# The experts' first layer with its weights standing in TensorE, and marks and gates made ahead

## The reference, cut to what matters

```python
gate_logits = einsum('bnd,ed->ben', x, gate_query)
affinity = _sinkhorn(gate_logits / exp(log_temp))      # 6 rounds
gates, idx = top_k(affinity, CAP)                      # CAP = 64 tokens for each of 16 experts
expert_in = take_along_axis(x[:, None], idx[..., None], axis=2)
h = gelu(einsum('becd,edf->becf', expert_in, w1) + b1[None, :, None, :])   # FF = 1024
expert_out = einsum('becf,efd->becd', h, w2) + b2[None, :, None, :]
out = zeros_like(x).at[batch, idx].add(gates[..., None] * expert_out)
```

## Time and profile before

| | |
|---|---|
| Median of 3 runs | 1174.94 us (1174.15 to 1175.01) |
| The profiled execution's own time | 1175.17 us |
| Its span, first to last instruction | 1173.4 us |
| Mean granted clock of TensorE | 0.976 |
| Busy: PE, DVE, ACT, POOL | 94%, 73%, 61%, 13% |

### The profile page before, as it was taken

How to read it: one execution, slowest core, us unless ns; L and a number is a source line. 1 busy time by engine, 2 the same in 40 slices (tenths; PEclk the granted TensorE clock), 3 DMA queues, 4 the chain that set the end, 5 groups by cost and what they waited for, 6 DMA issues and landing times.

```text
span 1173.4 us, 30372 instructions
## 1 busy us (share of the span) xinstructions
PE 1105.5 (94%) x12600; PEld 525.7 (45%) x12600; DVE 860.9 (73%) x2017; ACT 718.2 (61%) x823; POOL 151.4 (13%) x260
## 2 busy tenths in 40 slices
PE   4788999999999999999999999999999999888997
PEld 2443433332432323544454456555555552467554
DVE  4888565487788878889788889788878980378631
ACT  0345567887678867677776877677785789310111
POOL 3024125112111011000001000010001000000522
PEclk9898999999999989999999999999999999998999
DMA  5113408722011000103232200111102000088696
GB/s 168 32 36 95 117 16 152 169 36 74 25 35 40 16 15 2 53 28 88 79 101 65 88 18 28 52 47 30 30 20 65 17 16 2 24 310 193 184 345 173
DMA packets 81562, 90.45 MB, mean 77 GB/s; under 512 B 18208, under 2 KB 73952, under 8 KB 81424
## 3 DMA queue, kind: packets, MB, share of 16 engines
q1 hardware_dynamic: 75264, 80.04, 23.9%
q10 hardware_dynamic: 4368, 6.29, 1.7%
q0 software_dynamic: 1792, 2.16, 1.0%
HBM read 73.42 MB, written 15.04 MB: 75 GB/s over the span
## 4 chain that ended last, share of the span: by engine, by line
PE 76%; DVE 11%; DMA 5%; issue 4%; ACT 2%; POOL 1%; ACTq 0%; DVEq 0%; POOLq 0%
PE po L1778 24%; PE g L1886 16%; PE scores L1754 15%; PE scores L1758 6%; PE g L1871 3%; PE g L1831 2%; ACT probs L1194 2%; DMA out<-self_region,idx_scatter 1%; DVE mx L1465 1%; PE g L1821 1%; PE g L1861 1%; DMA out<-wo_sb,idx_scatter 1%; PE scores L1787 1%; DMA out<-wxq_sb,idx_scatter 1%; PE g L1977 1%
## 5 line engine op out<-in xcount | busy, mean ns | idle before, releaser
L1194 ACT ACTIVATE probs<-scores 128x1024 f32<-128x1024 f32 (+2 forms) x736 | 677.0, 968 | 239.7 <-PE scores L1754 131.3
L1465 DVE TENSOR_REDUCE mx<-g 128x1 f32<-128x400 f32 (+1 forms) x1024 | 526.4, 567 | 86.2 <-PE g L1886 76.6
L1886 PE MATMUL g<-cross_region,even_region 96*32 96x400 bf16 (+1 forms) x4096 | 310.5, 338 | 0.4
L1754 PE MATMUL scores<-even_region,cross_region 99*32 99x512 bf16 (+1 forms) x3264 | 255.0, 379 | 2.5 <-ACT probs L1194 2.5
L1778 PE MATMUL po<-probs,cross_region 128*32 128x512 f32 (+1 forms) x1664 | 225.3, 594 | 0.8 <-ACT probs L1194 0.8
L1886 PEld LDWEIGHTS g<-cross_region,even_region 96*32 96x32 bf16 x4096 | 123.3, 95 | 182.9 <-DVE mx L1465 81.9
L1778 PE MATMUL po<-probs,self_region 128*32 128x512 f32 (+3 forms) x1280 | 152.1, 550 | 4.5 <-POOL probs L1055 3.9
L1754 PEld LDWEIGHTS scores<-even_region,cross_region 99*32 99x32 bf16 (+1 forms) x3264 | 100.9, 96 | 96.0 <-issue 42.6
L1758 PE MATMUL scores<-self_region 36*128 36x512 bf16 (+3 forms) x640 | 104.9, 360 | 7.2 <-ACT probs L1194 6.8
L1055 POOL TENSOR_SCALAR_AFFINE_SELECT probs<-probs 128x256 f32<-128x256 f32 x128 | 58.8, 468 | 276.7 <-ACT probs L1194 275.9
L1022 POOL TENSOR_TENSOR rstd<-mv,half 128x1 f32<-128x1 f32 x48 | 26.7, 556 | 518.5 <-DVE mv L1273 518.3
(11 more groups left out here) (287 smaller groups left out, 881.3 us busy)
## 6 DMA issues: line engine op xcount, KB each, us to landing
cross_region<-in_w SPq DMA_DIRECT2D x16, 1024.0 KB, 12.8
even_region<-xq_d SPq DMA_DIRECT2D x192, 64.0 KB, 2.3
self_region<-in_w ACTq DMA_DIRECT2D x6, 1024.0 KB, 6.6
self_region<-in_w SPq DMA_DIRECT2D x6, 1024.0 KB, 13.8
cross_region<-xk_d SPq DMA_DIRECT2D x24, 200.1 KB, 8.0
xb<-in_x SPq DMA_DIRECT2D x32, 128.0 KB, 2.8
xb<-x_d SPq DMA_DIRECT2D x32, 128.0 KB, 2.4
probs<-in_w SPq DMA_DIRECT2D x4, 1024.0 KB, 13.2
```

The source lines that it names most:

```text
L1194: act.activation(probs[0:rows, s % 4, :, off:], ps[s % 2][0:rows, :, off:], ACT.Exp, scale=LSCALE if QUADS[n][0] == "self" else 1.0).then_ ...
L1465: dve.reduce_max(mx[:, k % 2, b, h, c:c + 1], g[:, 0:n_keys], AX_X).then_inc(g_free, 1)
L1754: mm = pe.matmul(ps[s % 2][c:c + n_keys, a, :], k_cross[0:NS * DH + 3, h, i * P + c:i * P + c + n_keys], rhs, start=True, stop=True)
L1886: mm = pe.matmul(g[q:q + 32, 0:n_keys], q_max[k % 2][0:NS * DH, h, b * P + q:b * P + q + 32], k_cross[0:NS * DH, 4 * (k % 4) + h, start:st ...
```

## The change

- `hidden(i, e)`: a 128x128 block of W1 stands in the array, and the 64 tokens of one expert stream. The output comes turned, with hidden numbers on the partitions, straight into the score bank `ps[i % 2]`. `turn_hidden` is gone.
- VectorE adds the bias from the score bank to `h_sb` in one 128x1024 instruction, with the bias on the partitions (`b1_t`); ScalarE's GELU reads `h_sb`. All biases come in one load, turned once by TensorE and copied.
- Marks: one bf16 comparison of 128x1024 for all pairs, summed by two matmuls of 512 columns. The token numbers' sums come from eight matmuls right after `tops`. `read_sums` runs once, over all pairs, and the first layer of pair 0 waits for it.
- Gates: the best values go through the same six shift steps as the token numbers, two of them ahead of the inputs, four spread between; a matmul adds the chunks up. The store of affinities and eight gathers are gone.
- `keep_busy` goes from 15 to 18 calls ahead of `best_t` and from 12 to 17 ahead of `tops`, with single ones later.
- In round i the merge of pair i−1 now stands between the two experts of the first layer. `next_w1` waits for the first layer's matmuls.

```diff
@@ tail order
-        tail += ["aff", "best_t", "cand_a", "cand_b", "limit", "sums", "tops", ("xe", 0), ("xe", 1), ("h", 0, 0), ("h", 0, 1), ("xe", 2),
-                 ("h", 1, 0), ("h", 1, 1)]
+        tail += ["aff", "best_t", "cand_a", "cand_b", "limit", "sums", "tops", "b1", ("xe", 0), ("xe", 1), ("xe", 2), "gates"]
...
@@ SP
-            for i in range(NB1):
-                if b1_sb[i] is b1_sb[-1]:
-                    sp.wait_ge(g_full, g_at(("gate", TB - 1)) + 1)
-                load_b1(i)
+            sp.dma_start(b1_rows, b1.rearrange("e (f n) -> (e f) n", n=P)).then_inc(b1_loaded, 16)
...
-            sp.wait_ge(router_pe, 3 + SINK_ITERS)
-            sp.dma_start(affin_d.rearrange("(b p) e -> p b e", p=P), affin[:, :, :]).then_inc(affin_stored, 16)
...
-                sp.wait_ge(g_free, TF["h", i, 1])
-                if i + NB1 < E // 2:
-                    load_b1(i + NB1)
+                sp.wait_ge(h_turned, i + 1)
@@ ScalarE
-                act.activation(h_t[i % 2], ps[i % 2][:, :, :].rearrange("p a b -> p (a b)"),
-                               ACT.Gelu_apprx_tanh).then_inc(gelu_done, 1)
+                act.activation(h_t[i % 2], h_sb[i % 2], ACT.Gelu_apprx_tanh).then_inc(gelu_done, 1)
@@ VectorE
+            def mark_tokens():
+                dve.tensor_tensor(marks, row_no.unsqueeze(1).broadcast_to((P, E // 2, P)),
+                                  idx_f.unsqueeze(2).broadcast_to((P, E // 2, P)), ALU.is_equal).then_inc(marked, 1)
+
+            def read_sums():
+                dve.wait_ge(pair_sums, 2)
+                link(dve.tensor_tensor(mix[:, :, 0:CAP], ps[0][:, 0, :].rearrange("p (i n) -> p i n", n=CAP),
+                                       idx_f.unsqueeze(2).broadcast_to((P, E // 2, CAP)), ALU.is_equal))
+                counts_of = ps[1][:, :, :].rearrange("p a b -> p (a b)").rearrange("p (i n) -> p i n", n=P)
+                dve.scalar_tensor_tensor(out=unused, in0=counts_of, scalar=0.0,
+                                         in1=row_no.unsqueeze(1).broadcast_to((P, E // 2, P)), op0=ALU.is_equal,
+                                         op1=ALU.mult).then_inc(sums_read, 1)
...
             def hidden(i):
-                for f in range(2):
-                    g = tail_full(dve, ("h", i, f))
-                    dve.tensor_tensor(h_sb[i % 2][:, f * TILE:(f + 1) * TILE], g[:, :],
-                                      b1_sb[i % NB1][:, f * TILE:(f + 1) * TILE], ALU.add).then_inc(g_free, 1)
+                dve.wait_ge(h_turned, i + 1)
+                if i >= 2:
+                    dve.wait_ge(gelu_done, i - 1)
+                dve.tensor_tensor(h_sb[i % 2].rearrange("p (f e n) -> p f e n", f=8, e=2),
+                                  ps[i % 2][:, :, :].rearrange("p a (f e n) -> p (a f) e n", f=4, e=2),
+                                  b1_t[:, 2 * i:2 * i + 2, :].rearrange("p e f -> p f e").unsqueeze(3)
+                                  .broadcast_to((P, 8, 2, CAP)), ALU.add).then_inc(h_biased, 1)
...
+            mark_tokens()
+            for r in range(2):
+                link(dve.memset(shifted_v[r][:, 0:CAP], 0.0))
+            link(dve.scalar_tensor_tensor(out=shifted_v[0][:, CAP:2 * CAP], in0=row_no[:, 0:CAP], scalar=n_here,
+                                          in1=best_v, op0=ALU.is_lt, op1=ALU.mult))
+            link(move(shifted_v, 0))
+            link(move(shifted_v, 1))
+            g = tail_full(dve, "b1")
+            dve.tensor_copy(b1_t.rearrange("p n f -> p (n f)"), g[:, 0:P]).then_inc(g_free, 1)
+            dve.wait_ge(g_free, TF["b1"])
             expert_in(0)
             expert_in(1)
-            mark(4)
-            mark(5)
-            read_sums(0)
+            link(move(shifted_v, 2))
+            read_sums()
             hidden(0)
-            mark(6)
-            mark(7)
             expert_in(2)
-            read_sums(1)
+            for k in range(3, 5):
+                link(move(shifted_v, k))
+            move(shifted_v, 5).then_inc(values_ready, 1)
             hidden(1)
@@ TensorE
-            keep_busy(15)
+            keep_busy(18)
             g = tail_bank(pe, "best_t")
...
-            keep_busy(12)
+            keep_busy(17)
             g = tail_bank(pe, "tops")
...
+            for i in range(E // 2):
+                mm = pe.matmul(ps[0][:, 0, CAP * i:CAP * (i + 1)], same_expert[:, 2 * i:2 * i + 1].broadcast_to((P, P)),
+                               shifted[0][:, CAP:2 * CAP], start=True, stop=True)
+            mm.then_inc(pair_sums, 1)
...
+            def hidden(i, e):
+                n = 2 * i + e
+                pe.wait_ge(w1_loaded[n % NSLOT], 16 * (n // NSLOT + 1))
+                if e == 0:
+                    pe.wait_ge(g_free, TF["xe", i])
+                    if i >= 2:
+                        pe.wait_ge(h_biased, i - 1)
+                    else:
+                        pe.wait_ge(sums_read, 1)
+                w = slots[n % NSLOT][:, 0:2048].rearrange("p (k n) -> p k n", k=DK)
                 pt = ps[i % 2][:, :, :].rearrange("p a b -> p (a b)")
                 for f in range(8):
+                    for k in range(DK):
+                        mm = pe.matmul(pt[:, f * P + CAP * e:f * P + CAP * (e + 1)], w[:, k, f * P:(f + 1) * P],
+                                       x_et[i % 2][:, k, CAP * e:CAP * (e + 1)], start=(k == 0), stop=(k == DK - 1))
+                if e:
+                    mm.then_inc(h_turned, 1)
...
             for i in range(E // 2):
-                if i + 1 < E // 2:
-                    turn_hidden(i + 1)
-                if i:
-                    merge(i - 1)
                 if i + 3 < E // 2:
                     expert_in(i + 3)
                 if i + 2 < E // 2:
-                    hidden(i + 2)
+                    hidden(i + 2, 0)
+                if i:
+                    merge(i - 1)
+                if i + 2 < E // 2:
+                    hidden(i + 2, 1)
                 expert_out(i)
```

More of the change, by code:

```diff
@@ L54 @@
 CHUNK = T // NCH
-NB1 = 5
 NONES = 8
@@ L614, in decoder_layer @@
         chunk_base = late_region[:, P + 4 * E + NCH:P + 4 * E + NCH + 1]
-        picked_affin = late_region[:, 256:256 + E // 2 * E].rearrange("p (i e) -> p i e", e=E)
+        gates = late_region[:, 256:256 + E // 2]
+        shifted_v = [even_region[:, 2304 + 2 * CAP * r:2304 + 2 * CAP * (r + 1)] for r in range(2)]
         idx_gather = sb("idx_gather", [P, E // 2], U32)
@@ L691, in decoder_layer @@
         picked = sem("picked")
-        affin_stored = sem("affin_stored")
-        gates_gathered = [sem(f"gates_gathered{i}") for i in range(E // 2)]
+        values_ready = sem("values_ready")
         gathered = [sem(f"gathered{i}") for i in range(E // 2)]
-        b1_loaded = [sem(f"b1_loaded{r}") for r in range(NB1)]
+        b1_loaded = sem("b1_loaded")
+        h_biased = sem("h_biased")
         b2_loaded = sem("b2_loaded")
@@ L961, in _ @@
                 load_w2(sp, e)
[L963 to L967, removed]
-            for i in range(NB1):
-                if b1_sb[i] is b1_sb[-1]:
-                    sp.wait_ge(g_full, g_at(("gate", TB - 1)) + 1)
-                load_b1(i)
+            sp.dma_start(b1_rows, b1.rearrange("e (f n) -> (e f) n", n=P)).then_inc(b1_loaded, 16)
             for r in range(2):
                 sp.wait_ge(parts_stored[r], 16 * n_parts[r])
+            sp.wait_ge(g_full, g_at(("gate", TB - 1)) + 1)
             by_parity = b2.rearrange("(i e) d -> e i d", e=2)
@@ L1617, in _ @@
             for k in range(6):
[L1618 to L1621, removed]
+                last = move(shifted, k)
                 if k < 5:
@@ L1781, in values, with keep_busy @@
                 mm.then_inc(pv_done, 1)
-            def keep_busy(n):
+            def keep_busy(n, bank=ps[0][:, 0, 0:D]):
                 for _ in range(n):
-                    pe.matmul(ps[0][:, 0, 0:D], ident[:, :], xbo_sb[:, :], start=True, stop=True)
+                    pe.matmul(bank, ident[:, :], xbo_sb[:, :], start=True, stop=True)
             pe.wait_ge(const_ready, 5)
@@ L2004, in expert_out, with count_marks @@
                 mm.then_inc(g_full, 1)
-            def pair_sum(i):
-                pe.wait_ge(marked, i + 1)
-                pe.matmul(ps[i // 4][:, i % 4 // 2, i % 2 * 2 * P:(i % 2 + 1) * 2 * P], ones[:, :], marks[i % 2],
-                          start=True, stop=True).then_inc(pair_sums, 1)
+            def count_marks():
+                pe.wait_ge(const_ready, 17)
+                pe.wait_ge(marked, 1)
+                for half_of in range(2):
+                    mm = pe.matmul(ps[1][:, half_of, :], ones_b, marks[:, 4 * half_of:4 * half_of + 4, :],
+                                   start=True, stop=True)
+                mm.then_inc(pair_sums, 1)
             def merge(i):
@@ L2019, in merge @@
                 pe.matmul(po[:, 0:D], mix[:, i, :], y_sum[i % 2], start=True, stop=True).then_inc(merged, 1)
-            keep_busy(2)
```

(28 more changed lines are left out.)

87 lines of the change are left out of this document (27 added, 60 removed).

## The result

The changed kernel takes 1216.98 us, median of four runs (1215.34 to 1218.29), against 1174.66 us for the kernel before, measured beside it: 1.0367 times as long, 95% interval 1.035 to 1.0384. It is slower, as forecast, but by 42 us and not by 22.5, and it lies outside the forecast's range (1187 to 1208). The profiled execution took 1217.27 us, with a span of 1215.4 us; that of before 1175.17 and 1173.4.

What follows compares the result with a forecast made beforehand. TensorE was taken to bound the kernel at 8.67 us a round, the scatters close behind at 8.26; −1.2 + 2.8 + 1.7 + 6.4 + 12.8 = +22.5 us on 1175.17 gave 1197.7, forecast 1197 us, range 1187 to 1208.

Steps and rivals of the forecast that it cites:

- the clock: Before pair 0's first layer: the new wait idles TensorE about 3 us, charged half a stretch at half clock, +1.7 us.
- Rival 2: Experts' loop: streaming fills half of each 0.109 us, so first layers run at half clock, 1225 to 1253 us; chance 0.09.
- Affinities to tops: Ahead of the tops: three more filler calls hold the clock, so the limit's copy starts at about 1075.6, −1.2 us.
- Wait, tops to first layer: Pair 0's first layer waits until VectorE has read the sums, starting about 1095.4 instead of 1092.54: +2.8 us.
- Three first layers and one second, at full clock: Start of the experts, to the end of pair 0's second layer: 25.3 us instead of 18.9, +6.4 us.
- First layer: Each pair: 64 loads of 128 columns at 0.109 us, 6.98 us where 3.48 stood, +3.50 us.
- rival 1: First layer: 128-column loads hide at 0.053 us, scatters' 8.26 us then bounds the round, about 1171 us; chance 0.08.
- rival 3: First layer: loads overlap in part at about 0.08 us, 15 us less, about 1182 us; chance 0.05.
- A round: One TensorE round of the experts' loop: 8.67 + 3.50 − 0.94 (hidden-row turn gone) = 11.23 us.
- 5 x 2.56: Five rounds, from the end of pair 0's second layer to that of pair 5, each 2.56 us longer: +12.8 us.
- The last rounds: Last two rounds, which have no first layer: nothing charged, 0 to −0.9 us allowed for the turn.
- Bias, activation, transfers, gates: Experts' part: VectorE's bias and the activation are hidden two rounds ahead, DMA changes lie under other work; no charge.

Runs made afterwards that it cites:

- the first experiment: Changed kernel plus seven filler calls in TensorE's wait ahead of the first layer of pair 0: 1193.37 us on chip A, 1.0100 times before.
- the second and third experiment: Changed kernel streaming 128 token columns per W1 load, 1196.99 us; changed kernel loading only 64 of each block's 128 W1 columns, 1170.22 us; both chip A.
- the head: Changed kernel with first layer, hidden-row turn and bias broadcasts as before; marks, sums, gates, fillers stay changed: 1168.54 us (chip B), 1169.27 us (chip C).

## Why the prediction was wrong

**The step that failed** is the clock, in the forecast "I charge half a stretch at half clock: +1.7 us (0 to 3.5)". The wait of 3 us was foreseen, and that the clock would fall in it; what was not is how long it would stay down. I took its length from the earlier trace rows, whose windows of 3.40 us I read as whole stretches. The first of the two began earlier, as a stretch of the same trace of before shows, so half clock had lasted 6.8 and 3.4 us:

```profile
1065.60:1069.00 3.40, 3.03 (x13) 2.51 (x14) 2.82 (x10) 0.00 (x0) 0.00 (x0) 0.51 1.04 234
```

And I did not ask what ran in it there: mostly fillers of 256 moving columns. Here three first layers follow that move columns for only half of their time, and half clock lasts 47.8 us. The distance from the first layer's start to the end of the first second layer is 18.90 us before and 48.27 after; at full clock, in the first experiment, 25.87. So the clock cost 22.4 us, not 1.7. That the wait set it off is shown by filling it. That the thin stream kept it down is shown by the two streams that were not thin, 128 columns moved for 128 loaded and 64 for 64, which had it back in 5.4 and 5.3 us after the same wait.

Rival 2 ("the clock falls in the experts' loop", 1225 to 1253 us, 0.09) named half clock, but for the wrong cause and in the wrong place: the thin stream lowered no clock that was up, neither in the first experiment nor in the changed kernel's later rounds. The missing case was the two together, a fall in the wait and no recovery under a thin stream. From the rows of before it could have been priced (three first layers at twice 7 us and a second layer at half clock), but not decided.

**The other terms**, from the two traces on the first chip, whose spans differ by 42.0 us:

| Step | Forecast | Measured |
|---|---|---|
| Ahead of the change (affinities turned at 1056.15, 1055.06) | 0 | −1.1 |
| Affinities to tops, put down to the fillers in the forecast (30.27, 28.71) | −1.2 | −1.6 |
| Wait, tops to first layer (6.12, 8.81) | +2.8 | +2.7 |
| Three first layers and one second, at full clock (18.90, 25.87) | +6.4 | +7.0 |
| Half clock in them (25.87, 48.27) | +1.7 | +22.4 |
| Five rounds (43.35, 57.39) | +12.8 | +14.0 |
| The rest (18.6, 17.2) | 0 | −1.4 |
| Sum | +22.5 | +42.0 |

The steps run from start to start: the turn of the affinities, the tops, the first layer of pair 0, the end of its second layer, the end of the second layer of pair 5, the end of the span.

*First layer.* Right: its price is the load, 0.110 us for 128 f32 columns at full clock, as the earlier trace rows said and the second and third experiment show; rival 1 (0.053) and rival 3 (0.08) are out. At half clock the loads came 0.214 us apart. The rule of the Trainium skill (TensorE: Matmul & The Clock Gate, LDWEIGHTS) gives 107 ns for 128 columns; at full clock the trace agrees.

*A round* is 11.50 us, not 11.23. A full round of before is 8.72 us (1111.44 to 1120.16); the 8.67 is the mean with a last one that has no input to turn. So a round grew by 2.78 us and not by 2.56. By starts, 0.14 of the difference is the first layer (3.64 more, from 3.49 to 7.13, where the forecast had 3.50 more), 0.06 the merge (0.49 against 0.43), and 0.05 the second layer (3.60 against 3.55); the input's turn is 0.03 shorter. With the last round, which grew by 2.9, the step "5 x 2.56" was mis-sized by 1.2 us.

*The last rounds* gave back 1.4 us, more than the 0 to 0.9 allowed. Up to the start of the last merge it is only 0.3, since an idle 0.57 us of TensorE stands where part of the turn was. The last scatter is then issued 1.35 us after that merge starts (1208.51, 1209.86), where it was 1.91 (1165.35, 1167.26) with a scatter still under way ahead of it, and the span ends 5.5 us after it instead of 6.1.

*Bias, activation, transfers, gates:* hidden, as forecast. The chain holds none of them.

**What stays open.** Why, on two of the chips, TensorE's steps seem to reach VectorE and ScalarE up to 8 us late in the kernel before, and not in kernels without the gathers of the gates. In the three traces that have them, the last late step lands 3.9 to 4.0 us after POOL has issued its last such gather. That is a coincidence in time and shows no cause: the head that lacks the gathers differs in other things too, and taking only them away was run on a chip that has no late steps. Why the clock's fall ahead of the tops lasts 6.8 us in one trace of the kernel before, 3.4 in another and does not come in a third was not tried. Nor was a stream between the thin one and the full ones.

## What to carry to other kernels

When an f32 matmul's two operands are swapped, count the loads first. In these traces a load of 128 columns sets a spacing of 0.110 us and a stream of 128 columns one of 0.113, so with 64 columns moved for 128 loaded the load was the bound, and the first layer took twice its time. And when a wait is put ahead of matmuls that are bound by loads, fill it: the clock that fell in such a wait did not come back in 42 us of them, and seven filler calls were worth 23 us. To judge one part of a change, put the rest of it on the old form; here the head, without the new first layer, was the only gain.

## What the runs showed of the hardware

The same stream, 64 columns for each 128-column load, held a clock of 1.00 for 22 us after fillers and did not lift one of 0.50 in 42 us after an idle wait of 3.07 us. With as many columns moving as loaded (128 or 64) the clock was back 5.4 and 5.3 us after the start. f32 loads of 128 columns came 0.110 us apart at full clock and 0.214 at half, with 64 moving columns and, at full clock, with 128. And the kernel before, with the same instructions, ran between 1172 and 1182 us by the chip; its profiled executions on chips B and C lie 9 us apart, to which the late steps and the half clock after them add 11 on chip B, and other stretches take 2 off.
